# Four graph layers with experts: a raw ring of five places in layer 2, expert weights split within the product of layer 0, and expert numbers loaded behind the first turns

## The reference

```python
# layer 0
x = x + _L0_gnn_ref(_layernorm(x), adj, W)      # adj @ x / (deg + 1), then a linear step
x = x + _L0_ffn_ref(_layernorm(x), ...)         # 32 experts, hidden 64, one expert for each row (argmax)
# layer 1
x = x + _L1_gnn_ref(_layernorm(x), adj, ...)    # three products with the scaled adj and layer norms
x = x + _L1_ffn_ref(_layernorm(x), ...)         # 8 experts, hidden 512, two for each row, softmax weights
# layer 2
x = x + _L2_gnn_ref(_layernorm(x), adj, adj, ...)
#   sim = tanh(adj * adj), kept where adj > 0 (at most 700 to a row);  relu(sim @ (h2 @ W_gcn) + b_gcn)
x = x + _L2_ffn_ref(_layernorm(x), ...)         # 8 experts, hidden 512, the top two, relu
# layer 3: attention over the graph, four heads, then shared and gated experts
```

## Time and profile before

| what | us |
|---|---|
| median of 3 runs (2186.91 to 2188.19) | 2187.2 |
| the profiled execution | 2189.29 |
| its span, from the first to the last instruction | 2187.5 |
| layer 0: the product's last tile is split | 209.6 |
| layer 0: DVE's scale steps of the last tile begin | 227.60 |
| layer 0: ACT's last row copy ends | 231.26 |
| layer 0: gather indices ready, first gather | 262.9, 263.19 |
| layer 0: the experts' last results on PE | 352.4 |
| layer 2: PE's last of the 22 tiles ends | 1397.6 |
| layer 2: the experts' first turn on PE | 1438.03 |

### The profile page before, as it was taken

How to read it: one execution, slowest core, us unless ns; L and a number is a source line. 1 busy time by engine, 2 the same in 40 slices (tenths; PEclk the granted TensorE clock), 3 DMA queues, 4 the chain that set the end, 5 groups by cost and what they waited for, 6 DMA issues and landing times.

```text
span 2187.5 us, 41945 instructions
## 1 busy us (share of the span) xinstructions
PE 1881.4 (86%) x15580; PEld 1267.4 (58%) x15580; DVE 1518.4 (69%) x3199; ACT 1139.2 (52%) x2236; POOL 437.5 (20%) x517
## 2 busy tenths in 40 slices
PE   6999396999999999939985989679967999999777
PEld 3788253788887887836763877557752222222333
DVE  6877666677776667764668557545676889897564
ACT  7565386543343344426764555246754345454654
POOL 0000575000100113216742100057600000000000
PEclk9999688999999999969996999779988999999898
DMA  7998456579888879964768365433243343232000
GB/s 222 338 348 332 123 162 197 170 260 343 314 314 317 305 267 375 375 222 140 242 213 278 89 173 149 181 88 97 83 128 95 94 120 91 82 95 70 9 18 26
DMA packets 238298, 412.55 MB, mean 189 GB/s; under 512 B 20495, under 2 KB 189071, under 8 KB 219856
## 3 DMA queue, kind: packets, MB, share of 16 engines
q1 hardware_dynamic: 214836, 361.52, 49.1%
q0 software_dynamic: 13760, 39.68, 5.9%
q10 hardware_dynamic: 9504, 8.65, 1.2%
HBM read 316.02 MB, written 93.78 MB: 187 GB/s over the span
## 4 chain that ended last, share of the span: by engine, by line
PE 62%; DVE 18%; ACT 7%; DMA 4%; issue 4%; POOL 3%; SPq 0%; ACTq 0%; DVEq 0%; POOLq 0%
PE ps L2870 10%; PE ps L1098 8%; PE ps L1100 8%; PE ps L1099 7%; PE ps L2876 5%; PE ps L293 4%; PE ps L294 4%; PE ps L295 4%; PE ps L2518 3%; DMA BIG<-in_adj 2%; PE ps L2520 1%; DVE BIG L1667 1%; DVE bst L487 1%; PE ps L2491 1%; DVE BIG L3054 1%
## 5 line engine op out<-in xcount | busy, mean ns | idle before, releaser
L1098 PE MATMUL ps<-R,BIG 128*128 128x256 f16 (+1 forms) x1764 | 483.9, 274 | 3.0 <-ACT BIG L1562 2.4
L1100 PE MATMUL ps<-R,BIG 128*128 128x256 f16 (+1 forms) x1764 | 481.5, 273 | 0.0
L1099 PE MATMUL ps<-R,BIG 128*128 128x256 f16 x1764 | 481.2, 273 | 0.0
L2870 PE MATMUL ps<-BIG 128*64 128x452 f32 x1056 | 230.9, 558 | 18.8 <-DVE BIG L3054 16.5
L3054 DVE SCALAR_TENSOR_TENSOR BIG<-BIG 128x904 f32<-128x904 f32 x176 | 192.1, 1155 | 36.1 <-PE ps L2876 25.0
L1098 PEld LDWEIGHTS ps<-R,BIG 128*128 128x128 f16 x1764 | 171.1, 97 | 30.0 <-issue 2.7
L1099 PEld LDWEIGHTS ps<-R,BIG 128*128 128x128 f16 x1764 | 173.0, 98 | 21.1 <-issue 0.3
L1100 PEld LDWEIGHTS ps<-R,BIG 128*128 128x128 f16 x1764 | 171.3, 97 | 23.9
L2870 PEld LDWEIGHTS ps<-BIG 128*64 128x64 f32 x1056 | 64.4, 136 | 179.3 <-issue 134.0
L2940 ACT ACTIVATE BIG<-X,BIG 128x64 f32<-128x64 f32 x264 | 70.3, 337 | 166.7 <-PE ps L2876 166.7
L293 PE MATMUL ps<-X,BIG 128*128 128x256 f16 (+1 forms) x568 | 138.4, 256 | 5.2 <-ACT X L2542 4.3
(11 more groups left out here) (460 smaller groups left out, 4408.0 us busy)
## 6 DMA issues: line engine op xcount, KB each, us to landing
BIG<-adj_split SPq DMA_DIRECT2D x63, 1376.0 KB
BIG<-in_adjT SPq DMA_DIRECT2D x32, 1408.0 KB, 10.3
BIG<-in_adj SPq DMA_DIRECT2D x22, 1408.0 KB, 10.6
BIG<-in_adjT SPq DMA_DIRECT2D x66, 452.0 KB, 3.3
adj_split<-BIG SPq DMA_DIRECT2D x21, 1376.0 KB, 11.6
XX<-in_f SPq DMA_DIRECT2D x70, 256.0 KB, 8.7
experts_split<-XX SPq DMA_DIRECT2D x64, 256.0 KB, 4.8
BIG<-experts_split SPq DMA_DIRECT2D x16, 1024.0 KB, 12.8
```

What stands on the lines that cost most here:

```text
L1098: pe.matmul(out[:, 0:n], pr[:, 0, k, :], h[:, k, 0:n], start=start, stop=False)
L1099: pe.matmul(out[:, 0:D], pr[:, 0, k, :], l[:, k, 0:D], start=False, stop=False)
L1100: return pe.matmul(out[:, 0:n], pr[:, 1, k, :], h[:, k, 0:n], start=False, stop=stop)
L2870: pe.matmul(ps[rs, 2 * (h // 2) + c, 0:CW], self.G[:, u, h * HF:(h + 1) * HF], self.PT[:, u, h, cs], start=start, stop=stop)
```

## The change

It has these parts:

- Layer 2's raw ring has five places (`RAW`): the three in BIG, half of X2 and half of XX. The fourth is free when the high and low halves of the sixth pair of rows before the product are made, the fifth when the stage before is through. The square of every late tile is then five tiles ahead and the tanh four.
- In layer 2's product the logits of row 8 move from behind the short tile to k = 7 of the tile behind it, and `parts_out` moves on ACT behind the row copy of the same turn.
- Layer 0's expert weights come in four loads of 1 MB into four places that the product has given up (in X2, XX and behind the seventh slot of BIG), issued on SP ahead of the route's waits. ACT copies the first eight blocks during the product's last two tiles and the other eight behind it. The split halves go to BIG from slot 4 on, the matrix `selE` to the start of BIG. DVE waits for the whole split before it writes its one-hot matrices.
- The first comparison of `numbers` is made ahead of the wait for PE's lists (`lm`).
- Experts0: PE turns tiles 0 and 1 before it waits for the route's end, and loads its words one by one: one, then three behind the second hidden product, then one at every third tile. ACT loads three in its start and the others at every third tile. POOL gathers twelve tiles before the degrees' power and four more before the next weights' split; DVE's three steps for the degrees stand behind result 14.
- Experts: PE makes turns 0 and 1 before it waits for the route's end and loads its four words.

The diff, cut to its core (renamed places and unchanged lines are left out):

```diff
@@ -81,7 +81,8 @@
...
-SQUARE_AT = tuple(max(t - 5, LATE[j - 3]) if j >= 3 else t - 5 for j, t in enumerate(LATE))
+RAW = 5
+SQUARE_AT = tuple(max(t - 5, LATE[j - RAW]) if j >= RAW else t - 5 for j, t in enumerate(LATE))
@@ -473,9 +474,39 @@
...
+        class FirstWeights(Weights):
+            GROUP = 4
+            def __init__(self, src, hi, lo, n, width):
+                super().__init__(src, hi, lo, n, width)
+                self.raw = [X2[:, 256:2304], X2[:, SLOT:SLOT + 2048], XX[:, SLOT:SLOT + 2048], BIG[:, YG:YG + 2048]]
+                others[0] += 12
+            def sp(self, sp):
+                p0.st.wait(sp, "lo", KT)
+                for u in range(4):
+                    at = slice(4 * u * self.width, 4 * u * self.width + 4 * self.width)
+                    sp.dma_start(self.raw[u], self.src[:, at]).then_inc(WS[f"ld{u}"], 16)
+            def block(self, b):
+                return self.raw[b // 4][:, b % 4 * self.width:(b % 4 + 1) * self.width]
+            def act(self, act, first=0, last=None):
+                for b in range(first, self.n if last is None else last):
+                    act.wait_ge(WS[f"ld{b // 4}"], 32)
+                    act.activation(self.hi[:, self.at(b)], self.block(b), ACT.Copy).then_inc(WS["hi"], 1)
+            def pool(self, pool):
+                for b in range(self.n):
+                    pool.wait_ge(WS["hi"], self.base + b + 1)
+                    pool.tensor_tensor(self.lo[:, self.at(b)], self.block(b), self.hi[:, self.at(b)], ALU.subtract)\
+                        .then_inc(WS["lo"], 1)
...
-        F = {0: Weights(io["f0"], *fsplit(NF[0]), NF[0] // ST, ST)}
+        F = {0: FirstWeights(io["f0"], *fsplit(NF[0], 4 * SLOT), NF[0] // ST, ST)}
@@ -1329,6 +1360,8 @@
...
+                    if t in (KT - 2, KT - 1):
+                        F[0].act(act, 4 * (t - KT + 2), 4 * (t - KT + 2) + 4)
...
             def dve(self, v):
@@ -1728,20 +1761,35 @@
...
+            @staticmethod
+            def landed(j):
+                return ("d4", "d5", "d6", "d0", "d1")[j % RAW]
+            @staticmethod
+            def raw(j):
+                o, u = ORDER[LATE[j]], j % RAW
+                space = BIG[:, (4 + u) * SLOT:(5 + u) * SLOT] if u < 3 else (X2[:, SLOT:2 * SLOT], XX[:, 0:SLOT])[u - 3]
+                return space[:, 0:KT * wide(o)].rearrange("p (k c) -> p k c", k=KT)
             def sp(self, sp):
...
                 def raw(src, j):
-                    s.wait(sp, "lo", j - 2)
+                    if j == 3:
+                        self.flow.st.wait(sp, "hl", PR // 2)
+                    if j == 4:
+                        self.flow.st.wait(sp, "hl", PR)
+                        self.flow.st.wait(sp, "mm", PR)
+                    s.wait(sp, "lo", j - RAW + 1)
...
-                    sp.dma_start(aslot(4 + j % 3, o)[:, :, 0:cols], src[:, :, o * P:o * P + cols]).then_inc(s[f"d{4 + j % 3}"], 16)
+                    sp.dma_start(self.raw(j)[:, :, 0:cols], src[:, :, o * P:o * P + cols]).then_inc(s[self.landed(j)], 16)
...
                 def loads(src):
...
-                    free += [(LATE[j - 3] - 1 if j >= 3 else -3, 1, j) for j in range(len(LATE))]
+                    free += [(LATE[j - RAW] - 1 if j >= RAW else -3 if j < 3 else 1, 1, j) for j in range(len(LATE))]
@@ -1799,6 +1846,8 @@
...
+                        if t == AT + 1 and k == 7:
+                            rows.logits(pe, s, AT - 3)
@@ -1817,10 +1866,16 @@
...
-                        zero_tail(pool, s, LATE.index(AT))
+                        self.zero_tail(pool, LATE.index(AT))
+            def zero_tail(self, pool, j):
+                s = self.st
+                self.flow.st.wait(pool, "mm", PR)
+                s.wait(pool, "lo", j - RAW + 1)
+                pool.memset(self.raw(j)[:, :, NC - (KT - 1) * P:SHORT], 0.0).then_inc(s["zp"], 1)
...
             def tanh(self, act, j):
-                a = aslot(4 + j % 3, ORDER[LATE[j]])
+                a = self.raw(j)
@@ -1828,15 +1883,13 @@
...
-                pr, a = pslot(t % 4, ORDER[t]), aslot(4 + j % 3, ORDER[t])
+                pr, a = pslot(t % 4, ORDER[t]), self.raw(j)
...
             def act(self, act):
...
-                    if t == AT:
-                        parts_out(act, s, t % 2, D, 1)
@@ -1845,14 +1898,16 @@
...
+                    if t == AT:
+                        parts_out(act, s, t % 2, D, 1)
...
             def square(self, v, j):
-                s, a = self.st, aslot(4 + j % 3, ORDER[LATE[j]])
-                s.wait(v, f"d{4 + j % 3}", 16 * (j // 3) + 16)
+                s, a = self.st, self.raw(j)
+                s.wait(v, self.landed(j), 16 * (j // RAW) + 16)
@@ -1913,8 +1968,6 @@
...
-                else:
-                    F[0].sp(sp)
@@ -1983,15 +2036,14 @@
...
-                ahead = {"argmax": 0, "softmax": 0, "top2": 16}[self.kind]
-                F[self.i].act(act, 0, ahead)
+                if self.kind == "argmax":
+                    F[0].act(act, 8)
...
-                F[self.i].act(act, ahead)
@@ -2119,6 +2171,8 @@
...
+                if A == 1:
+                    v.wait_ge(WS["lo"], F[0].base + F[0].n)
@@ -2130,23 +2184,16 @@
...
+                G = self.G
+                size = [1, G, E]
+                cmp = R2[0:1, 4 * LG:4 * LG + G * E].rearrange("p (j e) -> p j e", e=E)
                 def numbers():
...
-                    G = self.G
-                    size = [1, G, E]
-                    cmp = R2[0:1, 4 * LG:4 * LG + G * E].rearrange("p (j e) -> p j e", e=E)
...
-                        link(v.tensor_tensor(cmp, iota[:, 0:G].rearrange("p (j o) -> p j o", o=1).to_broadcast(size),
-                                             ends[0:1, 0, :].rearrange("p (o e) -> p o e", o=1).to_broadcast(size), ALU.is_ge))
...
-                        S = G - PAIRS
-                        tile, odd = packed[:, 0:G, :], packed[:, G:G + S, :]
-                        link(v.tensor_copy(tile[:, PAIRS:G, :], iota[:, SINGLE:SINGLE + S].rearrange("p (j o) -> p j o", o=1)))
-                        link(v.tensor_scalar(tile[:, 0:PAIRS, :], iota[:, 0:PAIRS].rearrange("p (j o) -> p j o", o=1), 2.0, None, ALU.mult))
-                        link(v.tensor_scalar(odd, tile[:, PAIRS:G, :], odd_at[0:1, :], None, ALU.subtract))
-                        link(v.tensor_tensor(cmp, tile.to_broadcast(size), over(ends[0:1, 0, :]).to_broadcast(size), ALU.is_ge))
@@ -2165,6 +2212,16 @@
...
+                if A == 1:
+                    link(v.tensor_tensor(cmp, iota[:, 0:G].rearrange("p (j o) -> p j o", o=1).to_broadcast(size),
+                                         ends[0:1, 0, :].rearrange("p (o e) -> p o e", o=1).to_broadcast(size), ALU.is_ge))
+                else:
+                    S = G - PAIRS
+                    tile, odd = packed[:, 0:G, :], packed[:, G:G + S, :]
+                    link(v.tensor_copy(tile[:, PAIRS:G, :], iota[:, SINGLE:SINGLE + S].rearrange("p (j o) -> p j o", o=1)))
+                    link(v.tensor_scalar(tile[:, 0:PAIRS, :], iota[:, 0:PAIRS].rearrange("p (j o) -> p j o", o=1), 2.0, None, ALU.mult))
+                    link(v.tensor_scalar(odd, tile[:, PAIRS:G, :], odd_at[0:1, :], None, ALU.subtract))
+                    link(v.tensor_tensor(cmp, tile.to_broadcast(size), over(ends[0:1, 0, :]).to_broadcast(size), ALU.is_ge))
@@ -2199,6 +2256,9 @@
...
+            def root(self, v):
+                s = self.st
@@ -2238,9 +2298,13 @@
...
+        def expert_word(eng, E, w):
+            return eng.value_load(eid[0:1, w:w + 1], min_val=0, max_val=E ** PER[E] - 1)
         def expert_words(eng, E):
...
-            return [eng.value_load(eid[0:1, w:w + 1], min_val=0, max_val=E ** PER[E] - 1) for w in range(WORDS[E])]
+            return [expert_word(eng, E, w) for w in range(WORDS[E])]
...
         def expert_of(words, g, E):
@@ -2277,20 +2341,20 @@
...
-                for j in range(8):
+                for j in range(self.J):
...
-                deg.pool(pool)
-                W[1].pool(pool)
-                for j in range(8, self.J):
-                    gather(j)
+                    if j == 11:
+                        deg.pool(pool)
+                    if j == 15:
+                        W[1].pool(pool)
...
             def pe(self, pe):
-                after(pe, self.route, F[0])
+                after(pe, F[0])
...
-                W2 = BIG[:, 0:4 * self.hid].bitcast(F16).rearrange("p (h x) -> p h x", h=2)[:, :, 2 * self.hid:]
-                J, e, at, words = self.J, {}, {}, expert_words(pe, E0)
+                W2 = BIG[:, 4 * SLOT:4 * SLOT + 4 * self.hid].bitcast(F16).rearrange("p (h x) -> p h x", h=2)[:, :, 2 * self.hid:]
+                J, e, at, words = self.J, {}, {}, []
...
                 def turn(j):
@@ -2323,21 +2387,36 @@
...
+                def word():
+                    if len(words) < WORDS[E0]:
+                        words.append(expert_word(pe, E0, len(words)))
...
+                for z, n in self.route.done:
```

(32 more changed lines are left out.)

## The result

The changed kernel takes 2173.76 us (median of four runs, 2172.04 to 2175.30), the kernel before beside it 2187.69: a ratio of 0.9938, 95% interval 0.9925 to 0.9952. That is 13.9 us faster, where I forecast 27. Its profiled execution took 2174.94, its span 2173.1 against 2187.5.

The account below looks back on a forecast made before the run. TensorE's own stream and its waits for VectorE were taken as the bound. Layer 0's 9.1, layers 1 and 2's experts' 2.0 and 3.7, and the product's 12.2 sum to 27.0: 2160.2 us, own range 2154 to 2166, whole 2152 to 2176.

Parts of the forecast that it names:

- three signs: Wrong if layer 0's experts gap every third iteration, DVE's steps at 227 take 1 us, or product waits exceed 6 us.
- Layer 2's product: Five raw places and moved steps remove most of PE's waits and lost clock: 12.2 us of a 15.2 ceiling.
- Route of layer 0: POOL's weight splits end earlier, so the step behind PE's rank matmuls comes 4.4 us earlier.
- The tail: End of the product before layer 0's route: POOL's blocks delay DVE's last scale steps, costing 0.4 us.
- case (c): Rival: POOL and DVE collide more, four steps of 1.37 in the tail and 3.5 in the experts; 2168, chance 0.05.
- First result: Layer 0's experts: first result matmul at 275.0 instead of 282.86, a gain of 7.9 us.
- POOL's gather 16 and the splits: Layer 0's experts: PE waits 1.2 us for gather 16; DVE's splits meeting POOL's four weight splits cost 0.6 us.
- Words in the stream: Layer 0's experts: loading the remaining words inside the stream costs 1.0 us, bounds 0 and 6.6.
- Rival (a): Words in the stream cost in full: layer 0 loses 5.6 us more, 2165.8; chance 0.12.
- Layers 1 and 2's experts: Two turns ahead of the words start the experts earlier: 2.0 us in layer 1, 3.7 in layer 2.

Follow-up runs that it names:

- ring_only: The kernel before with only layer 2's product changed as in the changed kernel; 2174.25 us, ratio 0.9945 to the kernel before.
- f0_first: Changed kernel with the four loads of expert weights issued ahead of the store of the product's last tile; 2169.03 us in one run.
- w1_dve: Changed kernel with VectorE instead of POOL splitting layer 1's feature weights, one block behind each of results 16, 19, 22, 25; 2168.12 us, ratio 0.9915.
- best_stream: Changed kernel plus the edits of `f0_first` and `w1_dve`, and layers 1 and 2's second turn behind the first hidden product; 2158.95 us, ratio 0.987.
- words_pe_twice: `w1_dve` with TensorE loading each of the nine words in its stream twice; 82.6 us from first to last result, against 76.9.
- words_act_twice: `w1_dve` with ScalarE loading each of the ten words in its stream twice; 79.0 us from first to last result, against 76.9.
- f0_chain: Changed kernel with each of the four 1 MB expert-weight loads issued only when the one before has landed; 2174.45 us, ratio 0.9942.
- w1_late: Changed kernel with POOL's four splits of layer 1's feature weights moved behind the last gather; 2172.98 us, ratio 0.9936.

## Why the prediction was off

The mechanism of the largest term was right, the sign was right, and the sum was 27 where 13.9 came: the time lay within the whole range but outside the forecast's own, 2154 to 2166. What failed are three steps of layer 0: the words in the stream, the load in the tail, and DVE's split beside POOL's four. Two of the three signs that I named as showing it wrong came: late iterations at every third word, and DVE steps of 1 us in the tail. By its own steps:

- *Layer 2's product, 12.2.* Right, and somewhat small: 14.0, 1.4 us of waits left where I kept 3.0. The lost clock came back as I had counted it. `ring_only` carries it alone.
- *Route of layer 0, 4.4.* Right in itself, and somewhat small (5.3): L2153 stands right behind the rank matmuls.
- *The tail, 0.4.* Here the prediction failed first. I wrote that the loads "are issued ... (about 209.6) and are wanted by ACT from 215 on" and set no price on their being late. The first stood behind the 1.4 MB store issued just ahead on SP's queue and landed at 220.7. ACT stood 4.39 us, which moved POOL's blocks onto the small DVE steps of both last tiles. 4.7 us instead of 0.4; `f0_first` gives them back with one swap. The range's case (c), "four steps of 1.37 in the tail", had the price but not the cause.
- *First result, 7.9.* Right, and 1.9 too small: 9.8. Most of the difference is the first gather itself. I kept its 2.65 us; it takes 1.30 in each of the eighteen kernels with the changed layer 0, and 2.65 in the two with the old one. Why, no run shows.
- *POOL's gather 16 and the splits, 1.2 + 0.6.* Mis-sized: 4.0 (80.82 in the changed kernel less 76.87 in `w1_dve`). I took 0.6 for the collision "because each split is wanted an iteration later"; the split of tile 9 was held for 4.33 us, three iterations' worth. The bound of 3.54 was the value to take: that row was the same case. PE didn't wait for gather 16. The Trainium skill (SBUF — State Buffer, Who interferes with whom) was the rule that spoke against my value, and the trace agrees: DVE's split (286.03 to 290.36) ends 0.16 us behind the last of POOL's four (290.20). A row of four does not always hold DVE so long: in the tail, the one-column steps beside such a row took 1.0 to 1.1 us each, about one of the four (1.15). What makes the difference, no run shows.
- *Words in the stream, 1.0.* The largest error: 7.3 to 8.3. Rival (a), with its 6.6, was the right one. The Trainium skill (Advanced Engine Details and Errata, Engine Queue Depths) gives TensorE a queue of 64 instructions; that it would cover a word was my reading of it, and it was wrong. A second word at each place stopped TensorE's own stream for 0.63 us, in a stage where PE is busy 24.88 of 25 us once no word stands in it (325 to 350).
- *Layers 1 and 2's experts, 2.0 and 3.7.* Wrong in one step. I let the second turn go ahead of the words at no cost; its rows land 2.7 us behind the first's in layer 2 and 4.7 in layer 1, and the first hidden product stands behind it. Measured 0.1 and 1.2; with the second turn back, 3.2 and 2.6 against before.

Layer 0 so comes to 5.3 - 4.7 + 9.8 - 4.0 - 7.8 = -1.4 (7.8 is the middle of 7.3 and 8.3), against -1.6 measured at its last result. Rivals (a) and (c) both held. Together, by their prices of 5.6 and 7.8 on top of 2160.2, they give 2173.6, all but the measured 2173.76. But that closeness is partly luck: the gains that I had too small (0.9, 1.9 and 1.8 us) make up for what layers 1 and 2's experts lacked (1.9 and 2.5).

That layer 1's product takes back what layer 0 gains, which I held possible after reading the first traces, was refuted by `w1_dve`, whose gather in layer 1 started 6.0 us earlier, and by `best_stream`: 7.9 us earlier at layer 0's last result, 9.8 at layer 1's first gather. Nor does the loss of 1.6 us that is gone at that gather need a cause of its own: the stretch from the one to the other took 624.4 us before, 622.7 in the changed kernel and as much in `ring_only`, which has the old code there, and 620.8 to 624.8 over all twenty traces.

## What to carry to other kernels

When a load moves up, look at what is issued just ahead of it on the same queue: a store there is part of its latency, and a copy that waits for it holds up everything behind it on its engine. An instruction moved into the stream of the engine that sets the pace cost its full time there and took back all that its absence had given at the start: ask where that engine already waits, and for what. And a step moved ahead of another waits for its *own* inputs first: price the wait for its data, not only its duration.

## What the runs showed of the hardware

- A load of a word of expert numbers into a register on TensorE takes 0.3 us in its row and 0.66 from one to the next, and in the stream its price is not hidden (5.7 us for nine more, `words_pe_twice`). On ScalarE, busy 23.7 of 25 us in the same stage, ten more beside TensorE's cost 2.1 (`words_act_twice`).
- A 1 MB load alone took 4.9 to 5.3 us, and 9.75 behind a 1.4 MB store on the same queue (`f0_chain`).
- Four GpSimd subtractions in a row held one VectorE subtraction, 0.28 us elsewhere, for 4.33 and 3.44 us, until 0.16 us behind the last of the four both times (changed kernel, `w1_late`). One-column VectorE steps beside four others took 1.0 to 1.1 us each, 0.16 without them (`f0_first`).
- Layer 0's first gather on GpSimd took 2.65 us in both kernels with the old layer 0 and 1.30 in all eighteen others. The cause is open.
